# Two buffers for the copied down weights, a shorter run of unread products ahead of layer 1's slots, and eight row buffers in layer 2's routed stage

## The reference, cut to what matters

```python
# layer 2 (layer 1 is the same without the shared expert, with softmax weights)
shared = silu(xt @ Wg_s) * (xt @ Wu_s) @ Wd_s
scores, idx = jax.lax.top_k(sigmoid(xt @ W_router + routing_bias), 2)
scores = scores / jnp.sum(scores, axis=-1, keepdims=True)
g = jnp.einsum('th,ehi->tei', xt, Wg_r)
u = jnp.einsum('th,ehi->tei', xt, Wu_r)
combined = jnp.einsum('tei,eih,te->th', silu(g) * u, Wd_r, wts)
return shared + combined
```

## Time and profile before

| | us |
|---|---|
| median of 3 runs | 817.55 (816.5 to 820.42) |
| the profiled execution's own time | 818.61 |
| its span (first to last instruction) | 816.8 |
| TensorE busy with products | 715.4 (88% of the span) |
| layer 1's expert stage, about | 331 to 424 |
| layer 2's expert stage, about | 565 to 647 |

### The profile page before, as it was taken

How to read it: one execution, slowest core, us unless ns; L and a number is a source line. 1 busy time by engine, 2 the same in 40 slices (tenths; PEclk the granted TensorE clock), 3 DMA queues, 4 the chain that set the end, 5 groups by cost and what they waited for, 6 DMA issues and landing times. The chain is left out here.

```text
span 816.8 us, 16930 instructions
## 1 busy us (share of the span) xinstructions
PE 715.4 (88%) x6115; PEld 577.2 (71%) x6115; DVE 437.7 (54%) x1155; ACT 244.9 (30%) x624; POOL 308.8 (38%) x365
## 2 busy tenths in 40 slices
PE   7997798899999889989896898798998878979997
PEld 5785687788888768844475686675433745879997
DVE  3766967545434365656534655675684367532212
ACT  1132411355445043124502411243364035111120
POOL 2346441456664140234214224411453187253211
PEclk9997997899999999899998799798998979899999
DMA  9403004788886439645324802100463244256603
GB/s 361 193 14 48 5 1 143 246 243 240 240 236 192 139 81 413 243 143 186 113 74 106 317 2 46 19 2 33 121 199 102 67 71 199 81 199 234 236 17 106
DMA packets 76553, 116.60 MB, mean 143 GB/s; under 512 B 44023, under 2 KB 57528, under 8 KB 73528
## 3 DMA queue, kind: packets, MB, share of 16 engines
q1 hardware_dynamic: 65141, 90.95, 35.3%
q0 software_dynamic: 6912, 17.31, 6.7%
q10 hardware_dynamic: 4418, 7.26, 2.4%
HBM read 100.34 MB, written 15.16 MB: 141 GB/s over the span
## 5 line engine op out<-in xcount | busy, mean ns | idle before, releaser
L280 PE MATMUL ps<-const_sb 128*128 128x128 f32 x946 | 126.4, 294 | 5.7 <-DMA const_sb<-in_consts 4.8
L280 PEld LDWEIGHTS ps<-const_sb 128*128 128x128 f32 x946 | 121.2, 208 | 9.0 <-DMA const_sb<-in_consts 4.8
L1878 PE MATMUL ps<-l0e_xg_fm,l0e_ring 128*128 128x128 f32 x544 | 72.7, 277 | 6.3 <-ACT l0e_up_sb L1968 2.5
L1878 PEld LDWEIGHTS ps<-l0e_xg_fm,l0e_ring 128*128 128x128 f32 x544 | 67.6, 191 | 12.2 <-issue 7.7
L955 PE MATMUL ps<-x_fm,w_sb 128*128 128x296 f32 x208 | 54.5, 414 | 4.6 <-PEq L237 4.3
L2473 PE MATMUL ps<-l_w,const_sb 128*32 x132 | 48.8, 506 | 7.7 <-DMA l1e_own_gu<-in_l_experts 3.0
L308 POOL TENSOR_TENSOR norm_r<-norm_ve,const_sb 128x2 f32<-128x2 f32 (+1 forms) x27 | 19.5, 724 | 92.5 <-DVE norm_ve L301 68.2
L955 PEld LDWEIGHTS ps<-x_fm,w_sb 128*128 128x128 f32 x208 | 39.1, 190 | 17.5 <-issue 6.1
L1784 POOL DMA_INDIRECT l0e_y_scratch<-l0e_y_tm,l0e_rows_u x34 | 35.6, 1047 | 32.3 <-ACT l0e_y_tm L1992 28.2
L413 ACT ACTIVATE x_fm<-ps 128x256 f32<-128x256 f32 x35 | 12.5, 383 | 107.5 <-PE ps L389 107.4
L1769 POOL DMA_INDIRECT l0e_xg_tm<-x_scratch,l0e_rows_u x34 | 33.3, 979 | 23.5 <-PE ps L1842 10.1
(11 more groups left out here) (518 smaller groups left out, 1635.0 us busy)
## 6 DMA issues: line engine op xcount, KB each, us to landing
l0e_ring<-in_l_experts SPq DMA_DIRECT2D x34, 514.0 KB
l_w<-in_l_experts SPq DMA_DIRECT2D x1, 8704.0 KB, 27.4
expert_w<-in_l_experts SPq DMA_DIRECT2D x4, 2048.0 KB
l_more_w<-in_l_experts SPq DMA_DIRECT2D x4, 2048.0 KB
l1e_own_gu<-in_l_experts SPq DMA_DIRECT2D x11, 704.0 KB
l_w<-in_l_experts SPq DMA_DIRECT2D x1, 6144.0 KB, 18.8
l2e_own_gu<-in_l_experts SPq DMA_DIRECT2D x11, 512.0 KB
l0e_down_w<-in_l_experts SPq DMA_DIRECT2D x1, 4096.0 KB
```

The source lines that it names most:

```text
L280: pe.matmul(ps[:, bank, 0:P], ident, ident, start=True, stop=True)
L1878: mm = pe.matmul(ps[0:widths[m], which, m * P:(m + 1) * P], w_n[:, c:c + widths[m]], x_n[:, k, :], start=(k == 0), stop=(k == KT - 1))
```

## The change

There are three edits, all in `column_experts`.

1. `own_dn` gets a second buffer, in both layers. The copies of slot n go to buffer n % 2, and they wait for the down products of slot n - 2 in place of slot n - 1. VectorE and ScalarE issue them one step of their loops earlier: `copy_dn(n)` stands where `copy_dn(n - 1)` stood, with the same semaphore value to wait for.
2. The run of unread products ahead of layer 1's first slot is 22 long, not 40. Layer 2 takes the other branch of that `if`, and nothing in it changes by this edit.
3. In layer 2 `ROWS` is 8, and the row buffers are a tensor of their own. `hid_fm` moves to other columns of `row_sb` with it.

```diff
                 own_gu = sb(f"{tag}_own_gu", [P, G - 1, 2, GU], where=st)
-                own_dn = sb(f"{tag}_own_dn", [P, G - 1, MT * D], where=st)
-                xg_tm = row_sb[:, YS * D:(YS + ROWS) * D].rearrange("p (u d) -> p u d", d=D)
+                own_dn = sb(f"{tag}_own_dn", [P, G - 1, 2, MT * D], where=st)
+                xg_tm = row_sb[:, YS * D:(YS + ROWS) * D].rearrange("p (u d) -> p u d", d=D) if ROWS == 4 \
+                    else sb(f"{tag}_xg_tm", [P, ROWS, D], where=st)
...
                             list_rows()
-                            stay_awake(pe, 40)
+                            stay_awake(pe, 22)
                             turn(0)
...
-                            if 1 <= r <= NS:
-                                if r == 1:
+                            if 0 <= r < NS:
+                                if r == 0:
                                     act.wait_ge(s_expert, 1)
                                     act.wait_ge(s_all, all_ready)
                                 if r >= 2:
 
                                     act.wait_ge(s_down, S + r - 1)
                                 for c in mine["act"][1]:
-                                    theirs = held_by(act, r - 1, c)
-                                    act.activation(own_dn[:, c - 1, :], whole(theirs, GU, GU + MT * D), ACT.Copy)\
+                                    theirs = held_by(act, r, c)
+                                    act.activation(own_dn[:, c - 1, r % 2, :], whole(theirs, GU, GU + MT * D), ACT.Copy)\
                                         .then_inc(s_dn[c], 1)
...
                         def copy_dn(n):
                             for c in mine["dve"][1]:
-                                if n >= 1:
-
-                                    dve.wait_ge(s_down, S + n)
+                                if n >= 2:
+
+                                    dve.wait_ge(s_down, S + n - 1)
...
-                        for n in range(NS + 1):
-                            if n < NS:
-                                hidden(S + n)
-                                if n + 2 < NS:
-                                    copy_gu(n + 2)
-                            if n >= 1:
-                                copy_dn(n - 1)
+                        for n in range(NS):
+                            hidden(S + n)
+                            if n + 2 < NS:
+                                copy_gu(n + 2)
+                            copy_dn(n)
...
-                       dense=(l2_w[:, 0, :], s_l2w, 16, xn, "w_ln2"), source=x0n)
+                       dense=(l2_w[:, 0, :], s_l2w, 16, xn, "w_ln2"), source=x0n, ROWS=8)
```

More of the change, by code:

```diff
@@ L2238, in column_experts @@
         def column_experts(tag, held, w_in, E, top, H, R, gu_by, dn_by, after, ahead=(), bias=None, dense=None, source=None,
-                           diag_in=None):
+                           diag_in=None, ROWS=4):
             G = P // R
@@ L2246, in column_experts @@
             NT = NS * G
-            ROWS, YS = 4, 3
+            YS = 3
             S, first = (0, 0) if dense is None else (TILES, 1)
@@ L2512, in _ @@
                                                        hid_fm[:, e % 2, m * P + c * R:m * P + (c + 1) * R],
-                                                       own_dn[:, c - 1, m * D:(m + 1) * D] if c
+                                                       own_dn[:, c - 1, (e - S) % 2, m * D:(m + 1) * D] if c
                                                        else whole(whose[e - S], GU + m * D, GU + (m + 1) * D),
@@ L2713, in copy_dn @@
                             for c in mine["dve"][1]:
-                                if n >= 1:
-                                    dve.wait_ge(s_down, S + n)
+                                if n >= 2:
+                                    dve.wait_ge(s_down, S + n - 1)
                                 whose = experts[n, c] if (n, c) in experts else held_by(dve, n, c)
-                                dve.tensor_copy(own_dn[:, c - 1, :], whole(whose, GU, GU + MT * D)).then_inc(s_dn[c], 1)
+                                dve.tensor_copy(own_dn[:, c - 1, n % 2, :], whole(whose, GU, GU + MT * D))\
+                                    .then_inc(s_dn[c], 1)
                         dve.wait_ge(s_expert, 1)
```

## The result

| | before | after |
|---|---|---|
| median of the runs, us | 817.21 (813.83 to 829.76, 11 runs) | 811.49 (805.28 to 814.45, 11 runs) |
| ratio, 95% interval | | 0.9926 (0.9898 to 0.9954) |
| the profiled execution, us | 818.61 | 805.28 |

The change gains 5.7 us. The forecast was 13.75, so 803.8, and 811.49 lies outside its range. The direction was right, the size was not.

The account below looks back on a forecast made before the run. TensorE, busy 88% of the span, was taken as the bound, with savings in its waits and unread products. 4.05 + 4.84 + 4.86 + 0 = 13.75 us off the median 817.55 gave 803.8, range 799.8 to 808.5.

Parts of the forecast that it names:

- Part 1: Head of layer 1: 22 unread products, not 40, save 4.05 us, or 3.6 if a gather lands late.
- Part 2, layer 1: End of layer 1's slots: the second own_dn buffer removes waits of 1.44 and 2.19 us; L2527 starts 4.84 us earlier.
- Part 2, layer 2: End of layer 2's slots: the second own_dn buffer lets L2527 start 4.86 us earlier, at 634.38 in place of 639.24.
- Part 3: Layer 2's slots: eight row buffers gain 0, added DMA traffic cancelling against a freed later load; bounds -0.8 to +2.5 us.
- B: Rival: layer 2's gathers collide moderately with SyncE's loads, +2.5 us, so 806.3; chance 0.10.
- E: Rival: layer 2's gathers delay four or five loads, TensorE idles 3 us each, then runs half speed: +18, 821.8; chance 0.03.
- A: Rival: TensorE's clock falls elsewhere as gaps shift; 807.3 with two more falls, 801 with one or two fewer; chance 0.14.
- C: Rival: layer 1's head gives nothing, as an input of slot 0 comes only at 351; 807.9; chance 0.04.
- D: Rival: scatters, not products, bound the end of each layer's slots, costing 2 x 2.3 us, so 808.4; chance 0.07.
- F: Rival: change doesn't do what it says, e.g. own_dn copies stay last at the end; 0.04 with others.
- The 5.9 to 6.1: Sign: the gap from the last scatter to L2527 should stay at 5.9 to 6.1 us.
- my estimate from it: Layer 2, from the skill page's figure: 3.4 us a gather with issue, one up to 3 us late, sum 806.8.

Follow-up runs that it names:

- g4: Kernel before with only the run of unread products cut from 40 to 22, on the 800 kind: ratio 0.9953, 3.8 us less.
- e2: Kernel before with only the run of unread products cut from 40 to 22, on the 816 kind: ratio 0.9985, 1.2 us less.
- h3: Kernel before with 22 unread products and the second own_dn buffer, without the eight row buffers, 800 kind: ratio 0.9832, 13.5 us less.
- m1: Changed kernel (all three edits) but with layer 2's gathers only four ahead, against the kernel before, 816 kind: 801.96 us, ratio 0.9812.
- e4: Kernel before with only layer 2's eight row buffers, all filled ahead, 816 kind: ratio 1.0074, 6.0 us more.
- f2: Kernel before with only layer 2's eight row buffers in their own tensor, gathers only four ahead, 800 kind: ratio 1.0015.
- g1: Kernel before with only layer 2's row buffers changed, to six, not eight, 800 kind: ratio 0.9979.
- h2: Kernel before with only layer 2's eight row buffers, gathers only four ahead, 800 kind: ratio 1.0020, 1.6 us more.
- e3: Kernel before with only the second own_dn buffer, in both layers, 816 kind: ratio 0.9898, 8.3 us less.
- h1: Kernel before with only layer 2's eight row buffers, all filled ahead, 800 kind: ratio 0.9995, 0.4 us less.
- k1: Changed kernel, all three edits, against the kernel before, 800 kind: ratio 0.9840, 12.8 us less.
- f1: Kernel before with 22 unread products and the second own_dn buffer, without the eight row buffers, 800 kind: ratio 0.983, 13.6 us less.
- g2: Kernel before with layer 2's eight row buffers, each gather fetching 64 rows in place of 128, 800 kind: ratio 0.9991.
- g3: Kernel before with layer 2's eight row buffers, each gather fetching 128 rows of half the length, 800 kind: ratio 0.9974.
- e1: Changed kernel, all three edits, run again against the kernel before, 816 kind: ratio 0.9942, 4.7 us less.

## Why the prediction was right and wrong

**Part 1, right.** 4.05 forecast; 3.84 in the traces, 3.8 by g4. On the 816 kind e2 has 1.2, with 3.8 at the edge of its interval. The first gather was 0.18 late, as the lower bound of 3.6 allowed. What I hadn't seen is that the clock can fall in the head's run of unread products. With 22 of them it does so in three traces of eight (e2, h3, m1: 20.3 to 20.6 us for the stretch, where the others take 17.9 to 18.6), with 40 in four of twelve (e4, f2, g1, h2: 24.3 to 24.7, the others 21.9 to 22.4). So it comes with both, costs some 2 us, and made e2's trace look like half a gain.

**Part 2, layer 1, right.** 4.84 forecast, 5.01 found. Slot 9's scatter begins 402.58 - 400.35 = 2.23 behind its products (2.22 forecast), slot 10's at 404.59, and L2528 5.73 behind that (5.8 forecast). The fall of the clock behind the slots is gone. It had cost 1.11 us in the unread products (7.63 to 6.52), not 1.32: the prediction's 6.31 is counted from start to start and its 7.63 to the end of the last. Without the other edits (e3) the stretches from first transpose to L2528 are shorter by 5.4 us in layer 1 and 4.4 in layer 2.

**Part 2, layer 2, right in kind, 0.9 too large.** 4.86 forecast, 3.91 found from slot 10's first gate-and-up product on. I let slot 10's scatter begin 628.25 - 626.39 = 1.86 behind its products, when GpSimd is free. It begins 618.88 - 616.34 = 2.54 behind them, 0.68 more, since ScalarE's copy of the result, not GpSimd, is last. The gap from there to L2528 is 6.34, 0.21 more than the sum has. And the products wait 0.39 us for `hid_fm`, which I had read as not binding, though they begin only some 0.06 later than forecast.

**Part 3, the step that failed.** The train of eleven gathers was priced at 0. That was a balance between traffic and a freed load, with bounds of -0.8 to +2.5. On the 816 kind it costs 4.3 to 7.0 us in slots 0 to 3 of the traces and 6.0 by e4's ratio (2.9 to 9.1). With it the sum is 13.75 - 6.0 = 7.7, less 0.9 for layer 2's end 6.8, beside 5.7 measured. On the 800 kind the 0 was right (h1, -0.4), and the whole forecast with it: 12.8 for all three edits (k1), 13.6 and 13.5 without the third (f1, h3), against 13.75. That layer 2's end was 0.9 too large is hidden there by the width of the intervals.

The bounds were too narrow because I priced the gathers only by what they move. The trace of before held a warning, and I had passed over it: in layers 0 and 3 there are waits for TensorE whose releaser the profile can't name, one of 8.8 us among them. Layers 1 and 2 had none, with their gathers four ahead; with the train ahead, layer 2 has them where TensorE in turn waits for the engine that is held up.

**The rivals.** B and E named the right place and the wrong mechanism: in slots 1 to 3 no product waited for a load. E's second half was right, a longer idle time and then the clock at 0.50; it happened once in each of the three traces and not 4.5 times, so some 6 us and not 18. Of A, a fall of the clock did come elsewhere, in layer 2's slots, but behind a new wait and not because a gap had moved. C, D and F didn't happen: the head gains, and the gap from the last scatter to L2528 is 5.73 and 6.34. (The 5.9 to 6.1 that the prediction names as a sign doesn't come out of its own sum, which has 5.82 and 6.13.)

**The page of the Trainium skill** that I weighed (SBUF — State Buffer, "SBUF: two separate sides") spoke against the train, and the train was bad, but no run shows its reason at work. Beside VectorE's float32 copies (two in 1.46 us) the gathers take 0.94 to 1.35 us in e4, not 3.1, and no product in slots 1 to 3 waits for a row there. In the trace of before the gathers that overlap such a copy take 0.95 to 1.65 us, the others 0.89 to 1.22. The page's 3.1 us stands beside a copy whose length it doesn't give, so my estimate from it had no ground.

**Open.** What the two kinds of chip differ in, and by what way a train of GpSimd's indirect DMAs keeps TensorE's results from being seen. That descriptors, bytes or the number in flight matter was tried only where nothing stalls (g1, g2, g3), so it isn't known. Whether the kind belongs to the chip or to the time of a series isn't known either: one chip came twice, with g and k, and was of the 800 kind both times. That pacing avoids the stall rests on one series of six runs and one trace, beside e3 and e2, which gather four ahead as well; on m1's chip the full train wasn't run.

## What to carry to other kernels

Filling buffers as far ahead as they allow is no free insurance: where no consumer waits for them, gather only as far ahead as is needed, and let the consumer's progress pace the queue. Look at the waits whose releaser the profile can't name before pricing anything at nothing: here they marked the chips on which the train cost something. And compare an experiment with its counterpart on the same chip: two series here (f and g) seemed to bear out a theory on chips where its effect doesn't exist.

## What the runs showed of the hardware

- Two kinds of chip: the same kernel takes 816 to 817 us on one and 800 to 801 on the other, 2% apart. The traces of the first have 10 to 17 waits of up to 9.5 us whose releaser the profile can't name, those of the second none.
- On the first, ten gathers of 0.94 to 1.35 us back to back on GpSimd went with waits for TensorE of 1.7 to 5.5 us in three traces of three (of ScalarE in after, of ScalarE, VectorE and GpSimd in e1 and e4), while the DMA engines were busy at 0.41 in e4; on the second, eleven such gathers (h1) went with none.
- Behind an idle time of TensorE of 2.5 to 4.5 us its clock was granted at 0.50 in three traces of three, and a gate-and-up product then took 1.06 us where it took 0.61.
